# Graph kernel of four layers: the first product of each gather issued as two matmuls of 128 columns

## The reference, cut to what matters

```python
h = jnp.maximum(_layernorm(x, axis=-1), 0.0)
x = x + _L0_gnn_ref(h, adj, W, a)       # elu(softmax(masked scores) @ (h @ W))
x = x + _L1_gnn_ref(h, adj, K, bias)    # relu(D (A+I) D @ h @ K + bias)
x = x + _L2_gnn_ref(h, adj, K2)         # relu(A @ h @ K2), rows masked
x = x + _L3_gnn_ref(h, adj, W3)         # relu(h @ W3a + (A @ h)/deg @ W3b)
```

## Time and profile before

| | |
|---|---|
| median of 3 runs | 2560.43 us (2557.01 to 2562.32) |
| profiled execution, its own time | 2557.61 us |
| its span, first to last instruction | 2555.8 us |
| outside of the span | 1.8 us |
| mean granted TensorE clock | 0.993 |
| PE busy | 2482.3 us, 97% |
| PEld busy | 2135.8 us, 84% |
| DVE busy | 2021.0 us, 79% |
| ACT busy | 1397.8 us, 55% |
| POOL busy | 1224.1 us, 48% |

### The profile page before, as it was taken

The page is one execution under the profiler, slowest core; times in us unless marked ns, Lnnn a source line. Parts: engine busy times, 40 slices in busy tenths (PEclk is TensorE's granted clock), DMA queues, the critical chain, the costliest instruction groups (busy, mean ns, idle before and its releaser), DMA issues.

```text
span 2555.8 us, 40394 instructions
## 1 busy us (share of the span) xinstructions
PE 2482.3 (97%) x13094; PEld 2135.8 (84%) x13094; DVE 2021.0 (79%) x4373; ACT 1397.8 (55%) x2571; POOL 1224.1 (48%) x1607
## 2 busy tenths in 40 slices
PE   2799999999999999999999999999999999999998
PEld 2688888888888888888888888888888888888887
DVE  6788878888888888788888888888788878878853
ACT  3565555555555555555556555555555555555542
POOL 2545545544544544544544545445445455455431
PEclk8899999999999999999999999999999999999999
DMA  4112222222222222221221222222222222222210
GB/s 144 44 42 57 55 66 54 57 67 52 59 67 51 60 66 51 60 67 49 62 66 50 62 59 56 63 58 57 61 59 57 60 61 56 60 61 56 49 34 25
DMA packets 355889, 149.40 MB, mean 58 GB/s; under 512 B 279520, under 2 KB 320096, under 8 KB 355680
## 3 DMA queue, kind: packets, MB, share of 16 engines
q1 hardware_dynamic: 355680, 146.82, 22.8%
HBM read 81.13 MB, written 33.62 MB: 45 GB/s over the span
## 4 chain that ended last, share of the span: by engine, by line
PE 95%; DVE 1%; issue 1%; POOL 1%; ACT 1%; SPq 0%; DMA 0%; POOLq 0%; ACTq 0%; DVEq 0%
PE O L340 46%; PE T L340 35%; PE X L340 13%; POOL h_lo L832 0%; SPq L287 0%; ACT h L466 0%; DMA act_out<-w_all 0%; POOL xs L797 0%; DVE ht_lo L684 0%; DVE p_lo L663 0%; DVE scores L590 0%; DVE w_lo L580 0%; DVE ln_stats L608 0%; POOL ln_scale L818 0%; DVE t_lo L669 0%
## 5 line engine op out<-in xcount | busy, mean ns | idle before, releaser
L832 POOL TENSOR_TENSOR h_lo<-h,h_hi 128x512 fp32r<-128x512 f32 x384 | 541.0, 1430 | 356.5 <-ACT h_hi L472 356.5
L466 ACT ACTIVATE h<-xs,ln_bias,ln_scale 128x512 f32<-128x512 f32 x512 | 395.7, 810 | 436.7 <-POOL ln_bias L826 436.7
L340 PE MATMUL O<-w_hi,t_hi 128*128 128x512 f32 x1536 | 597.9, 389 | 0.0
L340 PE MATMUL O<-w_lo,t_hi 128*128 128x512 f32 x1536 | 597.7, 389 | 0.0
L340 PE MATMUL O<-w_hi,t_lo 128*128 128x512 f32 x1536 | 597.7, 389 | 0.0
L669 DVE TENSOR_TENSOR t_lo<-T,t_hi 128x512 fp32r<-128x512 f32 x512 | 347.0, 688 | 251.7 <-ACT t_hi L478 251.5
L478 ACT CAST t_hi<-T 128x512 fp32r<-128x512 f32 x512 | 297.3, 582 | 409.1 <-PE T L340 409.1
L797 POOL TENSOR_TENSOR xs<-xs,act_out 128x512 f32<-128x512 f32 x128 | 164.7, 1310 | 584.1 <-ACT act_out L505 549.0
L608 DVE BATCH_NORM_STATS2 ln_stats<-xs 128x6 f32<-128x512 f32 x512 | 329.1, 680 | 23.7 <-POOL xs L803 16.9
L340 PEld LDWEIGHTS O<-w_hi,t_lo 128*128 128x128 f32 x1536 | 288.3, 188 | 59.9
L340 PEld LDWEIGHTS O<-w_hi,t_hi 128*128 128x128 f32 x1536 | 288.4, 188 | 55.3 <-DVE t_lo L669 0.5
(11 more groups left out here) (96 smaller groups left out, 5045.1 us busy)
## 6 DMA issues: line engine op xcount, KB each, us to landing
xs<-x SPq DMA_DIRECT2D x64, 512.0 KB, 5.2
out<-xs SPq DMA_DIRECT2D x64, 512.0 KB, 3.5
h<-act_out SPq DMA_DIRECT2D x976, 32.0 KB, 1.9
a_raw<-adj_t SPq DMA_DIRECT2D x64, 256.0 KB, 2.7
a_rows<-adj SPq DMA_DIRECT2D x64, 256.0 KB, 2.7
wh_rows<-wh_dram SPq DMA_DIRECT2D x61, 128.0 KB, 4.3
xs<-w_all SPq DMA_DIRECT2D x6, 512.0 KB, 7.2
act_out<-w_all SPq DMA_DIRECT2D x2, 512.0 KB, 6.6
```

What stands on the lines that cost most here:

```text
L340: last = nc.tensor.matmul(psum, s, m, start=(start and n == 0 and i == 0), stop=(stop and n == len(pairs) - 1 and i == 2))
L466: nc.scalar.activation(h[:, k.odd, m], xs[:, k.xb, m], ACT.Relu, bias=ln_bias[:, k.quad, m:m + 1], scale=ln_scale[:, k.quad, m:m + 1], acc ...
L832: nc.gpsimd.tensor_tensor(h_lo[:, k.odd, m], h[:, k.odd, m], h_hi[:, k.odd, m].bitcast(F32), ALU.subtract).then_inc(h_lo_ready, 1)
```

## The change

The first product of a gather (f = 0, m = 0) had three matmuls of 256 columns, of which the first began the accumulation (`start=True`). Now its high-by-high matmul is issued as two of 128 columns, for the left and the right half of T[:, 0]; only the first of them has `start=True`. Both have the same stationary operand. The two others are as before, and so are the 21 matmuls that follow. The waits ahead of the product stay where they were.

```diff
+            def gather_first(psum, s_hi, s_lo, m_hi, m_lo):
+
+                for i, c in enumerate((slice(0, P), slice(P, N))):
+                    nc.tensor.matmul(psum[:, c], s_hi, m_hi[:, c], start=i == 0, stop=False)
+                nc.tensor.matmul(psum, s_hi, m_lo, start=False, stop=False)
+                return nc.tensor.matmul(psum, s_lo, m_hi, start=False, stop=False)
+
             def gather(k):
...
                             if f == 0:
                                 wait(pe, h_lo_ready, k.part(L012, NT, m))
+                            if f == 0 and m == 0:
+                                last = gather_first(T[:, f], h_hi[:, k.odd, m, c], h_lo[:, k.odd, m, c], m_hi[:, m],
+                                                    m_lo[:, m])
+                                continue
                             last = product(T[:, f], [(h_hi[:, k.odd, m, c], h_lo[:, k.odd, m, c], m_hi[:, m],
                                                       m_lo[:, m])], start=m == 0, stop=m == NT - 1)
```

## The result

The changed kernel takes **2565.10 us** (median of 8 runs, 2564.19 to 2567.77) against 2558.26 us for the kernel before (8 runs, 2557.01 to 2562.32): a ratio of 1.0024, with a 95% interval of 1.0015 to 1.0033, so 6.8 us slower. The forecast was 2580 us, 20 us slower. (The forecast started from 2560.43 us, a median of three runs; the median of eight is 2.2 us lower.)

A forecast was written before the change was run, and what follows sets the result against it. TensorE was taken to bound the kernel, without slack in the middle. 192 gathers x 0.102 us of exposed loads = 19.6 us, on a median of 2560.4 us, gave 2580 us; range 2573 to 2628 us.

The forecast's parts named there:

- What bounds the kernel: Between 140 and 2440 us TensorE has no slack; a longer stage lengthens the program unless a wait behind it shortens.
- The price of the split: At each gather's first product, loads pace both short matmuls: 0.102 us extra per gather, 19.6 us in all; chance 0.66.
- the transposes of the earlier trace: Eight transposes of 128 columns, each with its own load, take 0.110 us each; taken as the price of a load.
- Two distances of 0.11 us: Sign at the gather's head: short matmuls start 0.11 us apart, the high-by-low one 0.11 us after the second.
- if 0.06, the loads were never the limit: Sign in a gather's timeline: distances of 0.06 us at the short matmuls would mean loads don't pace them.
- The rival of slow short products: An fp32r matmul of 128 columns may take as long as 512: 0.336 us per gather, 64.5 us, 2625 us; chance 0.22.
- those of one or both loads hidden: Behind the first short matmul: one load hidden, 10.7 us, 2571 us, 0.06; both hidden or nothing changed, 2562 us, 0.06.
- 256 array cycles: Claimed time of a 128-column transpose at either clock (0.110 and 0.217 us), argued for slow short products.
- a line with a constant through both: From 512 to 256 columns the distance falls 0.109 us, so 128 columns alone were put at 0.0635 us.
- The wait for ht_lo: Ahead of `project_first`, 0.11 us per graph, 6.8 us; moves with the gather, so stays; if swallowed, 12.8 us left.
- Its low end, 2573: Lower end of the range 2573 to 2628 us, taking in a swallowed ht_lo wait and some spread of the median.

The follow-up runs named there:

- each of eight: High-by-high matmul of all 8 products of a gather split, against the changed kernel's single split: 2726.21 us, 168 us slower than before.
- the seven cuts: Against the kernel before, the gather's first high-by-high matmul split at 64, 96, 128, 144, 160, 192 or 224 columns: 6.8 to 24.2 us slower.
- The run with 192 and 320 columns: Against the kernel before, no gather split; last 512-column matmul ahead of each gather issued as 192, then 320 columns: 2571.78 us, ratio 1.0050.
- the cuts at 144 and 192: Gather's first high-by-high matmul split into 144 and 112, or 192 and 64 columns, instead of 128 and 128: 2567.29 and 2567.19 us.
- the halves of 256: Against the kernel before, no gather split; last 512-column matmul ahead of each gather issued as two of 256: 2555.93 us, ratio 0.9987.
- the cut at 320: Against the kernel before, no gather split; last 512-column matmul ahead of each gather issued as 320, then 192 columns: 2567.34 us, ratio 1.0036.

## Why the prediction was wrong in size

**What bounds the kernel.** Right. TensorE had no slack in the middle, and all runs moved with the lengths of its stages, to within 5 us.

**The price of the split.** Right in size; the distances by which it was to be seen came out otherwise. Forecast 2 x 0.110 - 0.118 = 0.102 us per gather; measured 0.106 at the head, 0.104 in the gather with the split at its end, 0.106 for each of eight. Loads of 0.108 to 0.111 us pace the short matmuls, as the transposes of the earlier trace rows had suggested. Two distances of 0.11 us were to show it; measured were 0.060 and 0.109, and the 0.05 us that the first lacks came in the third, 0.173 for 0.118. By the prediction's own words ("if 0.06, the loads were never the limit") the loads would be ruled out. They aren't: the profile records the start of a short matmul's successor once the columns are through, 0.029, 0.044, 0.060, 0.068, 0.075, 0.089 and 0.103 us for 64, 96, 128, 144, 160, 192 and 224 columns, and that is before its load can be done. So where a load is exposed, sum over the head, or read the starts of the loads; there a load starts up to 0.083 us behind the matmul ahead of it, and not with it as the earlier trace rows had it. A product of 128 columns of fp32r is not slow: 0.060 us is near its columns' own 0.057. The rival of slow short products falls, and so do those of one or both loads hidden: the seven cuts cost the same whatever columns they have. (The "256 array cycles" with which the slow rival was argued are 264 at 2.4 GHz and 260 at 1.2, from 0.110 and 0.217 us.)

**The step that failed.** "Extra per gather: 2 x 0.110 - 0.118 = 0.102 us", then "Sum: 192 x 0.102". It takes the 21 matmuls behind the first product as unchanged, without a reason: their change is the term that was put at nothing. They went from 0.1178 to 0.1133 us each, 21 x 0.0045 = 0.094 us back of 0.106. I had read 0.118 as the price of 256 columns; it is not. The columns alone cost 0.2267 / 2 = 0.1133. The 0.0045 above it was in the earlier trace rows to be seen, had I halved the price of 512 columns instead of drawing a line with a constant through both; what that left as a fixed cost was time that another rhythm doesn't pay. That the split of the change brings this rhythm, where four other cuts don't, could not be read from any row, and why it does is open.

**The stages behind.** Not foreseen: the stage of 512 columns behind a gather with a split takes 5.455 us instead of 5.440, its first three distances being 0.232, 0.232 and 0.231. Three of these are 0.045 us a graph. It doesn't come with the quick rhythm: behind the four cuts that leave the gather at 0.118 it is 5.462 us.

**The wait for ht_lo.** Partly right. The chain does start at the end of the gather, so what the gather grew was not swallowed. But the 0.015 us that the projection grew lies behind that start, and `project_first` became shorter by 0.013 us, 5.547 to 5.534: that much was swallowed. The run with 192 and 320 columns shows the same at a larger size: the projection ahead grew by 0.044 us, and the first distance of `project_first` fell by 0.047, from 0.305 to 0.258. Per graph: 3 x 0.011 + 3 x 0.015 - 0.013 = 0.065 us, against 38.60 - 38.53 = 0.07 measured; 192 / 3 graphs make 4.2 us. The runs' difference of 6.8 us is larger by some 2.6, within its interval (3.8 to 8.4). But the cuts at 144 and 192 have the same steady graph of 38.60 us and took 7.8 and 8.1 us more than before, with intervals that begin at 4.9. So something beside the steady graph costs a few us in all three. Their traces have three graphs each in the middle that are 0.2 to 1.0 us longer than the median, 1.1 to 1.8 us together, and the kernel before has none; what else belongs to it is open.

**The range.** Its low end, 2573, rested on the ht_lo wait alone. No rival let the rest of the gather become quicker. The two rivals on that side, at 2571 and 2562 us with 0.06 each, lay outside the range, and 2565.10 between them: the time came near theirs, but by neither of their reasons. With the split cut at 64, 96, 160 or 224 columns, or in the last product, the forecast of 2580 us would have been right within 4 us, in part by luck, since the stages behind were left out there too.

## What to carry to other kernels

A short matmul on a full TensorE costs the load behind it, about 0.11 us for a block of 128x128 in fp32r, whether it had 32 or 224 columns here; add this per split and don't expect a repeated stationary block to be free. Before summing a local change over a stream of matmuls that barely hide their loads, compare their distance with their columns' share of longer ones: a difference, here 0.0045 us, can be given back to all of them or not, and only a run tells which. Where it exists, look for a cheap way to get the quick rhythm, such as two halves of 256 columns ahead of the stream. Try it stage by stage: here it worked behind the projections and not behind `gather_last`.

## What the runs showed of the hardware

Streams of fp32r matmuls of 256 columns have two steady rhythms here at the full clock, 0.1178 and 0.1133 us per matmul, with the same instructions. A change of the matmuls ahead can turn one into the other in all steady gathers, but doesn't fix it: most kernels here hold single gathers in the other rhythm, many of them behind a wait. Matmuls of 512 columns take 0.2267 in a stream, but the first three to ten of a stage can stand 0.224 to 0.239 us apart, and the twelve into O of `gather_last` stand 0.226, 0.229 and 0.232 apart by turns, in the kernel before and in the changed one. What the two rhythms are inside the engine, no run here shows: an exposed load is neither needed (the halves of 256) nor enough (the cut at 320), and a block loaded twice in a row has no part in it. A load of 128x128 that nothing hides follows the one ahead after 0.108 to 0.111 us, in all seven cuts.
